# A decoder layer on one core: the MLP's first projection in 11 tiles for 12, with the entry to the feed-forward loop and its closing in a new order

## The reference

```
x = x + attention(norm(x))            # causal, 16 heads of 64
x = x + cross(norm(x), ctx)           # linear attention, 16 heads of 16
y = norm(x); then 2 layers:
    h = shift_token(y); q,k,v = h @ wqkv; l2norm, rotary, local attention (8 heads, window 128)
    y = y + o @ wo
    h = norm(shift_token(y)) * g + b
    h = h @ w1 + b1                   # 256 -> 2 x 682
    a, g = split(h);  h = a * gelu(g)
    y = y + h @ w2 + b2               # 682 -> 256
out = x + y
```

## Time and profile before

| | us |
|---|---|
| median of 3 runs | 1221.88 (1221.18 to 1222.47) |
| the profiled execution | 1221.09 |
| its span, first to last instruction | 1219.2 |
| granted TensorE clock, mean | 0.996 |

### The profile page before, as it was taken

The page is one execution under the profiler, slowest core; times in us unless marked ns, Lnnn a source line. Parts: engine busy times, 40 slices in busy tenths (PEclk is TensorE's granted clock), DMA queues, the critical chain, the costliest instruction groups (busy, mean ns, idle before and its releaser), DMA issues.

```text
span 1219.2 us, 20487 instructions
## 1 busy us (share of the span) xinstructions
PE 1158.6 (95%) x6672; PEld 887.5 (73%) x6672; DVE 843.6 (69%) x2443; ACT 686.5 (56%) x1696; POOL 592.3 (49%) x648
## 2 busy tenths in 40 slices
...
DMA packets 31628, 46.11 MB, mean 38 GB/s; under 512 B 4572, under 2 KB 19632, under 8 KB 31536
## 3 DMA queue, kind: packets, MB, share of 16 engines
...
...
## 4 chain that ended last, share of the span: by engine, by line
PE 56%; issue 20%; POOL 14%; DVE 7%; ACT 3%; DMA 0%; POOLq 0%; DVEq 0%; ACTq 0%
PE psum L1494 34%; POOL probs L658 14%; PE psum L1754 5%; PE psum L1803 5%; PE psum L1788 4%; PE psum L1770 4%; PE psum L1736 2%; ACT hnT_hi L974 1%; DVE lp L1353 1%; DVE ra L1309 1%; ACT hnT L974 1%; DVE rb L1315 1%; PE psum L1816 1%; DVE ss L1319 1%; DVE stats L1027 1%
## 5 line engine op out<-in xcount | busy, mean ns | idle before, releaser
L658 POOL TENSOR_TENSOR probs<-probs,rden 128x128 f32<-128x128 f32 (+3 forms) x256 | 177.6, 730 | 211.2 <-DVE rden L1088 211.2
L813 ACT ACTIVATE probs<-probs,negmax 128x128 f32<-128x128 f32 (+3 forms) x256 | 140.6, 554 | 22.6 <-DVE negmax L1083 22.6
L944 ACT ACTIVATE lp<-lp,lneg,rn 128x256 f32<-128x256 f32 (+1 forms) x256 | 143.8, 571 | 14.1 <-DVE lneg L1365 13.9
L1076 DVE CUSTOM_DVE_ANT_0 probs<-psum,causal 128x512 f32<-128x512 f32 (+3 forms) x256 | 110.0, 486 | 2.2 <-issue 0.8
L702 POOL TENSOR_TENSOR rn<-ss,neg_half 128x8 f32<-128x8 f32 x64 | 106.5, 1664 | 3.8
L1353 DVE CUSTOM_DVE_ANT_0 lp<-psum,local 128x256 f32<-128x256 f32 (+1 forms) x256 | 84.0, 384 | 25.6 <-PE psum L1754 25.6
L693 POOL TENSOR_TENSOR lp<-lp,lrden 128x768 f32<-128x768 f32 x64 | 95.0, 1484 | 0.0
L1494 PE MATMUL psum<-q,k_rest 128*128 128x256 f32 (+2 forms) x256 | 88.8, 358 | 4.3 <-DVE rowmax L1076 2.9
L1560 PE MATMUL psum<-ident,probs 128*128 128x128 f32 x640 | 91.0, 274 | 1.7 <-POOL probs L658 1.6
L1494 PE MATMUL psum<-w,hid 114*128 114x256 f32 (+1 forms) x384 | 85.5, 379 | 1.1 <-DVE hid L1421 1.1
L1494 PE MATMUL psum<-wqkv_hi,hT_lo 128*128 128x512 f32 x192 | 82.1, 428 | 4.1 <-DVE rb L1315 2.8
...
## 6 DMA issues: line engine op xcount, KB each, us to landing
k<-k_round SPq DMA_DIRECT2D x128, 128.0 KB, 2.3
...
```

What stands on the lines that cost most here:

```text
L658: ins = pool.tensor_tensor(pr, pr, rden[:, j % 2, h, i:i + 1].broadcast_to([P, TRI[i]]), ALU.mult)
L813: ins = act.activation(pr, pr, ACT.Exp, bias=negmax[:, j % 2, h, i:i + 1], scale=ADH ** -0.5, accum_out=den[:, j % 2, h, i:i + 1])
L944: ins = act.activation(pr, pr, ACT.Exp, bias=lneg[:, u % 2, h, w:w + 1], scale=rn[:, m % 2, w, 0, 2 * j + h:2 * j + h + 1], accum_out=lden ...
L1076: ins = dve.tensor_tensor_reduce(probs[:, j % 2, h, TRI_AT[i]:TRI_AT[i + 1]], bank[:, at:at + TRI[i]], causal[:, S - TRI[i]:S], 1.0, -3e38 ...
```

## The change

Tiles 0 to 3 get 124 hidden rows, tile 4 gets 122, tile 5 the last 64. For tile 5 gate and value are columns of one product: 64 gate rows land in partitions 0 to 63 of a bank, 64 value rows in 64 to 127. ACT writes Gelu of it to partitions 64 to 127 of gl; DVE reads value, bias and gl at 64 to 127 and writes hid at 0 to 63. The rows 64 to 127 of that tile in hid are set to zero once by POOL, in w2 they are zero from the host, and `second_part` contracts 128 rows there. w1's columns, b1 and w2 are laid out by tiles on the host. w2 is loaded with one DMA per layer. The strings of the entry and the closing are new; `STEP_*` is as it was.

```diff
-FT = -(-HID // NF)
-FL = HID - FT * (NF - 1)
+FHALF = P // 2
+FROWS = (124, 124, 124, 124, 122, FHALF)
+FAT = [sum(FROWS[:f]) for f in range(NF + 1)]
...
-        ENTRY_PE = ("awo.0 kv.0 awo.1 x1T.0 KV.0 xq.0 kv.1 awo.2 kv.2 x1T.1 KV.1 xo.0 xq.1 kv.3 xw.0 "
-                    "x1T.2 awo.3 xq.2 KV.2 xo.1 KV.3 x1T.3 xw.1 hT.0 xq.3 xo.2 q.0.0 k.0.0 q.0.1 k.0.1 "
-                    "v.0.0 q.0.2 k.0.2 xw.2 Tqk.0.0 v.0.1 xo.3 Tqk.0.1 v.0.2 q.0.3 k.0.3 v.0.3 hT.1 xw.3 "
...
-                    "Tqk.1.2 v.1.3 Sb.3 hT.2 AV.1 T.2.0 q.2.0 Tqk.1.3 k.2.0 T.2.1 Sa.4 Sb.4 AV.2 T.3.0 "
-                    "q.2.1 k.2.1 T.3.1 v.2.0 Sa.5 AV.3 Sb.5 wo.0.0 wo.0.1 T.4.0 Sa.6 sh.0 T.4.1 v.2.1 "
+        ENTRY_PE = ("awo.0 kv.0 awo.1 x1T.0 KV.0 xq.0 kv.1 x1T.1 awo.2 kv.2 xo.0 KV.1 xq.1 x1T.2 kv.3 "
+                    "xw.0 awo.3 xq.2 KV.2 KV.3 xo.1 x1T.3 xw.1 xo.2 hT.0 xq.3 q.0.0 k.0.0 v.0.0 q.0.1 "
+                    "xw.2 k.0.1 v.0.1 q.0.2 k.0.2 Tqk.0.0 v.0.2 q.0.3 Tqk.0.1 k.0.3 xo.3 v.0.3 hT.1 xw.3 "
...
+                    "Sa.3 AV.1 Sb.3 Tqk.1.2 hT.2 T.2.0 q.2.0 Tqk.1.3 k.2.0 T.2.1 Sa.4 Sb.4 q.2.1 AV.2 "
+                    "T.3.0 v.2.0 T.3.1 k.2.1 Sa.5 AV.3 Sb.5 wo.0.0 wo.0.1 T.4.0 Sa.6 sh.0 T.4.1 v.2.1 "
...
-                     "kv.2 norm2.2 KV.1 keys.2 xq.1 kv.3 qadd.1 xw.0 keys.3 kvs.1 awo.3 y.0 xq.2 norm2.3 "
-                     "qadd.2 KV.2 KV.3 kvs.2 xw.1 hT.0 xq.3 weights.0 tab.0 q.0.0 k.0.0 qadd.3 q.0.1 "
-                     "kvs.3 k.0.1 Tqk.0.0 q.0.2 k.0.2 y.1 xw.2 Tqk.0.1 q.0.3 k.0.3 hT.1 xw.3 Tqk.0.2 "
-                     "q.1.0 Tqk.0.3 Sa.0 k.1.0 Sb.0 Sa.1 tab.1 soft.0.0 Sb.1 soft.0.1 q.1.1 T.0.0 T.0.1 "
-                     "soft.1.0 Sa.2 k.1.1 Sb.2 Tqk.1.0 soft.1.1 q.1.2 soft.2.0 y.2 T.1.0 k.1.2 Tqk.1.1 "
-                     "T.1.1 Sa.3 q.1.3 Tqk.1.2 k.1.3 hT.2 Sb.3 T.2.0 soft.2.1 y.3 soft.3.0")
+                     "kv.2 norm2.2 KV.1 keys.2 kv.3 xq.1 xw.0 qadd.1 keys.3 y.0 awo.3 kvs.1 xq.2 norm2.3 "
+                     "qadd.2 KV.2 KV.3 kvs.2 xw.1 weights.0 hT.0 xq.3 tab.0 q.0.0 k.0.0 q.0.1 qadd.3 xw.2 "
+                     "k.0.1 Tqk.0.0 q.0.2 kvs.3 k.0.2 q.0.3 y.1 Tqk.0.1 k.0.3 hT.1 xw.3 Tqk.0.2 q.1.0 "
+                     "Tqk.0.3 k.1.0 Sa.0 q.1.1 Sb.0 tab.1 Sa.1 Tqk.1.0 soft.0.0 Sb.1 soft.0.1 k.1.1 T.0.0 "
+                     "q.1.2 soft.1.0 T.0.1 Sa.2 y.2 k.1.2 soft.1.1 Tqk.1.1 Sb.2 T.1.0 q.1.3 Sa.3 T.1.1 "
+                     "soft.2.0 k.1.3 soft.2.1 y.3 Tqk.1.2 Sb.3 hT.2 soft.3.0 T.2.0")
...
-                     "exp.2.1 hT.2 AV.1 T.2.0 exp.3.0 Tqk.1.3 exp.3.1 q.2.0 k.2.0 v.1.3 T.2.1 AV.2 T.3.0 "
-                     "q.2.1 exp.4.0 T.3.1 k.2.1 AV.3 w1_parts.0 exp.4.1 v.2.0 T.4.0 exp.5.0 T.4.1 exp.5.1")
...
+                     "Tqk.1.2 AV.0 AV.1 hT.2 exp.3.0 T.2.0 Tqk.1.3 q.2.0 exp.3.1 k.2.0 w1_parts.0 T.2.1 "
+                     "q.2.1 T.3.0 exp.4.0 T.3.1 AV.2 k.2.1 AV.3 v.2.0 exp.4.1 T.4.0 exp.5.0 T.4.1 exp.5.1")
...
-        CLOSE_PE = ("T.29.0 hnT.6 T.29.1 Sa.31 w1.6.0 Sb.31 w1.6.1 AV.29 T.30.0 w1.6.2 T.30.1 w1.6.3 "
-                    "AV.30 T.31.0 w1.6.4 T.31.1 wo_early.7.0 AV.31 wo_early.7.1 wo.7.0 wo.7.1 w1.6.5 "
+        CLOSE_PE = ("T.29.0 hnT.6 T.29.1 Sa.31 w1.6.0 Sb.31 AV.29 T.30.0 w1.6.1 T.30.1 w1.6.2 AV.30 "
+                    "T.31.0 w1.6.3 w1.6.4 T.31.1 wo_early.7.0 AV.31 wo_early.7.1 wo.7.0 wo.7.1 w1.6.5 "
                     "sh.7 w2.6.0 hnT.7 w2.6.1 w1.7.0 w1.7.1 w1.7.2 w1.7.3 w1.7.4 w1.7.5 w2.7.0 w2.7.1")
...
-                     "stats.7 w1.6.5 norm.7 apply.7 w2.6.0 hnT.7 w2.6.1 w1.7.0 w1.7.1 w1.7.2 w1.7.3 "
+                     "stats.7 w1.6.5 norm.7 apply.7 hnT.7 w2.6.0 w2.6.1 w1.7.0 w1.7.1 w1.7.2 w1.7.3 "
...
-        CLOSE_POOL = ("bias.6 soft.30.1 soft.31.0 sum.0 soft.31.1 norm.7 sum.1 bias.7")
+        CLOSE_POOL = ("soft.30.1 sum.0 soft.31.0 bias.6 soft.31.1 norm.7 bias.7 sum.1")
...
                 turn(("w1g", *at), "g")
-                turn(("w1a", *at), "g")
+                if at[1] < NF - 1:
+                    turn(("w1a", *at), "g")
+                else:
+                    plan["w1a", at[0], at[1]] = plan["w1g", at[0], at[1]]
...
+            def zero_hidden():
+
+                wait_full(pool, plan["xw", B - 1, 1])
+                pool.memset(hid[:, NF - 1, :], 0.0).then_inc(hid_zero, 1)
...
+                if f < NF - 1:
+                    act.activation(gl[0:rows, f % GELU_T, :], bank[0:rows, :], ACT.Gelu, bias=bias)\
+                        .then_inc(read[use[0]], 1)
+                else:
+                    act.activation(gl[FHALF:P, f % GELU_T, :], bank[0:FHALF, :], ACT.Gelu, bias=bias)\
+                        .then_inc(last_gate, 1)
...
+                else:
+                    bank = wait_full(dve, use)
+                    dve.wait_ge(last_gate, m + 1)
+                    if m == 0:
+                        dve.wait_ge(hid_zero, 1)
+                    at = slice(FHALF, P)
+                dve.scalar_tensor_tensor(hid[0:rows, f, :], bank[at, :], b1[at, m // B, 0, f:f + 1],
+                                         gl[at, f % GELU_T, :], ALU.add, ALU.mult).then_inc(read[use[0]], 1)
...
-                for what, lo in (("w1g", HID + f * FT), ("w1a", f * FT)):
+                for what in ("w1g", "w1a") if f < NF - 1 else ("w1g",):
+                    rows = FROWS[f] if f < NF - 1 else P
+                    lo = 2 * FAT[f] + (rows if what == "w1a" else 0)
...
```

More of the change, by code:

```diff
@@ L28 @@
 NF = 6
-FT = -(-HID // NF)
-FL = HID - FT * (NF - 1)
+FHALF = P // 2
+FROWS = (124, 124, 124, 124, 122, FHALF)
+FAT = [sum(FROWS[:f]) for f in range(NF + 1)]
+assert FAT[NF] == HID
 W = 128
@@ L195, in build @@
         gl = sbt(ctx, "gl", [P, GELU_T, S])
-        hid = sbt(ctx, "hid", [FT, NF, S])
+        hid = sbt(ctx, "hid", [P, NF, S])
         loT = sbt(ctx, "loT", [P, FPAIRS, S])
@@ L255, in build @@
         w_hi, w_lo = sem("w_hi"), sem("w_lo")
+        hid_zero, last_gate = sem("hid_zero"), sem("last_gate")
         w1_hi_ok, w1_lo_ok = sem("w1_hi_ok"), sem("w1_lo_ok")
@@ L308, in build @@
         UNITS = STEPS * FPAIRS
-        ENTRY_PE = ("awo.0 kv.0 awo.1 x1T.0 KV.0 xq.0 kv.1 awo.2 kv.2 x1T.1 KV.1 xo.0 xq.1 kv.3 xw.0 "
[7 rows of a table removed]
-        ENTRY_DVE = ("awo.0 kv.0 norm2.0 keys.0 awo.1 xq.0 KV.0 qadd.0 kv.1 norm2.1 keys.1 kvs.0 awo.2 "
[6 rows of a table removed]
-        ENTRY_ACT = ("keys.0 x1T.0 xq.0 keys.1 qadd.0 x1T.1 keys.2 xo.0 xq.1 keys.3 x1T.2 qadd.1 xq.2 "
[6 rows of a table removed]
-        ENTRY_POOL = ("norm2.0 norm2.1 kvs.0 norm2.2 y.0 kvs.1 norm2.3 kvs.2 weights.0 y.1 q.0.0 k.0.0 "
[4 rows of a table removed]
+        ENTRY_PE = ("awo.0 kv.0 awo.1 x1T.0 KV.0 xq.0 kv.1 x1T.1 awo.2 kv.2 xo.0 KV.1 xq.1 x1T.2 kv.3 "
[7 rows of a table added]
+        ENTRY_DVE = ("awo.0 kv.0 norm2.0 keys.0 awo.1 norm2.1 xq.0 KV.0 qadd.0 kv.1 kvs.0 keys.1 awo.2 "
[6 rows of a table added]
+        ENTRY_ACT = ("keys.0 x1T.0 xq.0 x1T.1 qadd.0 keys.1 xo.0 keys.2 xq.1 keys.3 qadd.1 x1T.2 xq.2 "
[6 rows of a table added]
+        ENTRY_POOL = ("norm2.0 norm2.1 kvs.0 norm2.2 y.0 kvs.1 norm2.3 weights.0 kvs.2 y.1 q.0.0 k.0.0 "
[4 rows of a table added]
         STEP_PE = ("v2@1 hnT@-1 q2@1 Ta1 k2@1 Tb1 Sa3 hid0@-1 Tqk1@1 hid1@-1 Sb3 hid2@-1 hid3@-1 q3@1 "
@@ L352, in build @@
                      "fa2@1 q3@2")
-        CLOSE_PE = ("T.29.0 hnT.6 T.29.1 Sa.31 w1.6.0 Sb.31 w1.6.1 AV.29 T.30.0 w1.6.2 T.30.1 w1.6.3 "
-                    "AV.30 T.31.0 w1.6.4 T.31.1 wo_early.7.0 AV.31 wo_early.7.1 wo.7.0 wo.7.1 w1.6.5 "
+        CLOSE_PE = ("T.29.0 hnT.6 T.29.1 Sa.31 w1.6.0 Sb.31 AV.29 T.30.0 w1.6.1 T.30.1 w1.6.2 AV.30 "
+                    "T.31.0 w1.6.3 w1.6.4 T.31.1 wo_early.7.0 AV.31 wo_early.7.1 wo.7.0 wo.7.1 w1.6.5 "
                     "sh.7 w2.6.0 hnT.7 w2.6.1 w1.7.0 w1.7.1 w1.7.2 w1.7.3 w1.7.4 w1.7.5 w2.7.0 w2.7.1")
-        CLOSE_DVE = ("soft.27.1 Tqk.7.3 T.26.1 Sa.28 Sb.28 T.27.0 w2.5.0 soft.28.0 T.27.1 Sa.29 Sb.29 "
[4 rows of a table removed]
+        CLOSE_DVE = ("Tqk.7.3 T.26.1 Sa.28 T.27.0 soft.27.1 Sb.28 w2.5.0 soft.28.0 T.27.1 Sa.29 T.28.0 "
[4 rows of a table added]
                      "w1.7.4 w1.7.5 w2.7.0 w2.7.1")
-        CLOSE_ACT = ("AV.28 T.29.0 hnT.6 exp.30.0 T.29.1 exp.30.1 w1.6.0 w1.6.1 exp.31.0 AV.29 T.30.0 "
-                     "w1.6.2 T.30.1 exp.31.1 w1.6.3 AV.30 T.31.0 T.31.1 w1.6.4 AV.31 w1.6.5 hnT.7 w1.7.0 "
+        CLOSE_ACT = ("T.29.0 AV.28 hnT.6 exp.30.0 exp.30.1 T.29.1 w1.6.0 AV.29 T.30.0 exp.31.0 T.30.1 "
+                     "w1.6.1 w1.6.2 exp.31.1 AV.30 T.31.0 w1.6.3 T.31.1 w1.6.4 AV.31 w1.6.5 hnT.7 w1.7.0 "
                      "w1.7.1 w1.7.2 w1.7.3 w1.7.4 w1.7.5")
-        CLOSE_POOL = ("bias.6 soft.30.1 soft.31.0 sum.0 soft.31.1 norm.7 sum.1 bias.7")
+        CLOSE_POOL = ("soft.30.1 sum.0 soft.31.0 bias.6 soft.31.1 norm.7 bias.7 sum.1")
         MLP = ("stats", "sh", "norm", "apply", "hnT", "hT", "bias")
@@ L981, in gates @@
                     wait_read(act, plan["w1a", m, f - GELU_T])
-                rows = frows(f)
```

(20 more changed lines are left out.)

38 lines of the change are left out of this document (24 added, 14 removed), and 28 rows, old and new, of tables (CLOSE_DVE, ENTRY_ACT, ENTRY_PE, ENTRY_POOL).

## The result

The changed kernel takes 1213.18 us (median of 4 runs, 1212.38 to 1215.67), the kernel before 1222.18 beside it (4 runs, 1221.18 to 1222.5). The ratio is 0.9934 (0.9919 to 0.9948): 0.7% faster. I had said 1209.5 us, range 1204 to 1215. The profiled execution went from a span of 1219.2 to 1211.8 us, 7.4 less where I had 12.4.

The account below looks back on a forecast made before the run. The prediction took PE to bound the feed-forward loop and DVE the entry. Loop and closing 10.4 us plus entry 2.0 made 12.4, so 1221.9 us would fall to 1209.5, range 1204 to 1215.

Parts of the forecast that it names:

- The tiles: Feed-forward loop: 11 first-projection products per step for 12, 1.39 us each; loop and closing together gain 10.4 us.
- POOL's swap: Closing: batch 1's final sum on POOL moves behind step 7's bias, so DVE's hn runs shorter; 0.5 us gain.
- rival 3: First projection: wider weight loads set the matmul pitch, so 6.3 us come back, 1215.8 us; chance 0.02.
- rival 4: Merged tile: the serial chain ends later, w2 waits, 6 to 10 us come back, 1215.5 to 1219.5; chance 0.08.
- The closing: Last steps: gains of 1.9 us at m = 6 and 0.74 at m = 7; up to 1 us of loss allowed.
- The entry: Entry, 537 to 631 us: the reordered queues gain 2.0 us, bounds minus 2 and 8.
- the walk along DVE: Entry: DVE's new order walked with its present durations; xw.3 ends at 575.7 for 578.54, 2.8 us earlier.
- ACT's part, the split: Entry: ACT waits 0 to 2 us for w1's load before splitting it; 1.0 us charged.
- The wait of 1.88 us: Entry: DVE's wait for Tqk.0.0, to vanish because xw.2 is done before k.0.1.
- rival 1: Entry neutral: what DVE saves comes back as waits; 1211.5 to 1213 us; chance 0.22.
- rival 2: Entry gives most of DVE's idle time, 5 to 8 us, with a steadier clock; 1203.5 to 1206.5; chance 0.14.

Follow-up runs that it names:

- e6: The changed kernel with ACT's split of w1 back behind AV.3, as in the kernel before; ratio 0.9936 to the kernel before.
- e7: e5 with y.1 also moved on DVE, behind kvs.3; ratio 0.9975 to the kernel before.
- e5: The changed kernel with y.3 moved back on DVE behind T.2.0, as before; 1217.42 us, ratio 0.9971 to the kernel before.
- e1: The changed kernel (11 tiles, new closing) with the four entry strings of the kernel before; 1207.76 us, ratio 0.9898.
- e8: The kernel before (12 products) with only the four new closing strings; 1220.12 us beside 1220.9, ratio 0.9997.
- e12: e3 with PE's one wait of 2.56 us near 550 us filled with 16 transposes of the identity; 1206.84 us, ratio 0.9883.
- e3: e1 with second_part waiting for tiles 4 and 5 only ahead of their own matmuls; 1206.65 us, ratio 0.9886.
- e4: The kernel before (12 products, old closing) with only the four new entry strings; 1223.95 us, ratio 1.0029.
- e9: The changed kernel with T.1.1 ahead of Sa.3 and hT.2 ahead of Sb.3 on DVE, to shorten two PE waits; ratio 0.9928.

## Why the prediction was right or wrong

1. **The tiles: right.** e2, 11 tiles with nothing else, is 10.4 us below before at equal clock; the sum has 9.9 without POOL's swap. The full step is 78.33 us for the 78.35 said, six matmuls take 1.48 between starts (853.37 to 854.85, of which 0.08 is the start after another kind of work), weights of 124 columns change nothing, so rival 3 is out. With the waits at 0.46, 0.33 and 1.83 us for 0.55, 0.44 and about 1.7, rival 4 is out too.
2. **The closing: right.** hn of step 7 comes 0.47 us earlier behind the shift product (0.5 said), w2.7.0 0.77 us (0.74 said). The rest of the 4.1 us is the fall of the clock in the one profiled execution of before, which I had as PE's plain speed. A walk on one execution takes over what was chance in it.
3. **The entry: wrong, in sign.** The step that failed is the walk along DVE ("2.8 us earlier"), and with it what hangs on it, "so the entry gives 2.0". ACT's part, the split, was harmless: it waited for nothing, and e6 puts it back for 0.2 us. The walk said xw.3 would end at 575.7; it ended at 578.74, for 578.54 before. Timeline of DVE in the kernel after (to the earlier trace rows):
```profile
549.52 2.38 DVE L1258 TENSOR_TENSOR qT<-qr,qm 128x512 f32<-128x512 f32 x2
...
557.51 0.68 DVE L1342 COPY lkT<-psum 128x512 f32<-128x512 f32 x1
...
568.23 2.41 DVE L1049 TENSOR_SCALAR y<-x,mv,rstd 128x256 f32<-128x256 f32 x4
570.56 0.68 DVE L1342 COPY lkT<-psum 128x512 f32<-128x512 f32 x1
...
578.74 0.66 DVE L1342 COPY lkT<-psum 128x512 f32<-128x512 f32 x1
```
DVE lost its wait of 1.88 us, but two of its items grew. qadd.3 (the rows qT<-qr,qm) took 2.38 us for 1.29 and y.1 2.41 for 1.38, and a new wait of 0.61 us for PE came inside xw.3. From q.0.0 to the end of xw.3 that is 2.7 us more against 1.9 less: 37.7 us for 36.8. Timeline of DVE before:
```profile
547.34 1.29 DVE L1245 TENSOR_TENSOR qT<-qr,qm 128x512 f32<-128x512 f32 x2
...
563.69 1.38 DVE L1036 TENSOR_SCALAR y<-x,mv,rstd 128x256 f32<-128x256 f32 x4
```
Beside both POOL now runs a sum of two 128x512 tiles, where it had a power of 128x8. Timelines of POOL, after and before (y.1's neighbour):
```profile
549.53 1.82 POOL L699 TENSOR_TENSOR ra<-ra,rb 128x512 f32<-128x512 f32 x1
...
568.24 1.28 POOL L699 TENSOR_TENSOR ra<-ra,rb 128x512 f32<-128x512 f32 x1
```
```profile
563.85 1.75 POOL L702 TENSOR_TENSOR rn<-ss,neg_half 128x8 f32<-128x8 f32 x1
```
The Trainium skill, page "SBUF — State Buffer", section "Who interferes with whom", has this: DVE and GpSimd share a pair of ports, and one of the two stands still while the other holds it; it names DVE instructions in a two-port mode, and those with two inputs in SBUF against a GpSimd instruction that reads there. By this rule, the trace agrees: qT has two such inputs, and the 1.09 and 1.03 us more are within POOL's 1.82 and 1.28. That y runs in a two-port mode no view shows. The runs bear out the neighbour as the cause. In the 14 profiles, between 500 and 640 us, 23 single instructions of y take over 1 us beside such a sum, and each ends 0.15 us after it. In e7, which is e5 with y.1 moved to where POOL has a power, y.1 takes 1.37 us for 2.41. The walk kept every duration as it was in the old neighbourhood.

The wait of 1.88 us, which the new order was to remove, was itself chance. In the profile of the kernel before, PE's products ahead of Tqk.0.0 ran at the low clock for a while, 0.43 us apart (timeline of PE, kernel before):
```profile
551.41 0.63 PE L1494 MATMUL psum<-wqkv_lo,hT_hi 128*128 128x512 f32 x1
551.84 0.63 PE L1494 MATMUL psum<-wqkv_hi,hT_hi 128*128 128x512 f32 x1
```
In e1, e8 and e12, with the same order and a clock of 1.00 from 534 to 580, DVE waits 0.28 or 0.29 us there. Timeline of DVE in e1:
```profile
556.58 0.69 DVE L1342 COPY lkT<-psum 128x512 f32<-128x512 f32 x1 [0.29 <-PE psum L1757]
```
From q.0.0 to the end of xw.3 the old order takes 34.6 us in these three profiles and 36.8 in those of the kernel before, e2 and e3, where the clock fell; the new order takes 37.0 to 38.4 in its seven. So it never gained what the old order had with a full clock.
4. **What the sum left out: the clock.** At equal clock the new entry costs 0.8 us with 12 tiles (e4, give or take 0.5) and 0.6 with 11 (changed kernel against e1, give or take 1.1); that is rival 1, a neutral entry, or slightly worse. (The changed kernel was timed where the kernel before took 1.2 us more than beside e1, so its 0.6 may be less; e6 and e9, with nearly its orders, are 0.8 and 1.1 above e1.) The rest of 4.4 and 3.5 us goes with the mean clock, 0.9898 for 0.9965 and 0.9915 for 0.9947: 4.8 and 2.3 us by the slope, which is an estimate. The earlier trace rows had 0.98 in the entry; I used it only as a possible gain (rival 2) and gave no case to a loss.
5. **The total.** 1219.0 to 1208.0 at equal clock is 11.0 us, between rival 1's 10.4 and the forecast's 12.4; the clock takes some 3.5 of it, and the runs beside each other give 9.0 by the medians and 8.1 by the ratio. The time lies in the range because the range had room for a neutral entry and small misses. That the clock would take this room was not foreseen, so the range was hit partly by luck.
